# Low halves in VectorE's waits, a row normalised by ScalarE, and eight places of TensorE's side chain moved: a two-layer graph kernel

## The reference

```
q = x[sub] @ Wq.T + bq ; k = x[obj] @ Wk.T + bk          # 8 heads of 64
att[h, e] = (q * k).sum over head h / 8
scores = zeros ; scores[:, sub, obj] = att
scores = where(adj == 0, -inf, scores) ; diagonal = 1e-7
A = softmax(scores, axis=2).sum over heads / 8
x = layernorm(x + A @ x)
x = layernorm(x + adj @ (x @ weight) + bias)
```

## Time and profile before

| what | value |
|---|---|
| median of 3 runs | 165.84 us |
| lowest, highest | 165.1, 166.38 us |
| profiled execution: its own time | 166.42 us |
| profiled execution: span, first to last instruction | 164.7 us |
| busy, share of the span: PE, DVE, ACT, POOL | 93%, 77%, 45%, 43% |
| granted TensorE clock, mean | 0.994 |

### The profile page before, as it was taken

The page is one execution under the profiler, slowest core; times in us unless marked ns, Lnnn a source line. Parts: engine busy times, 40 slices in busy tenths (PEclk is TensorE's granted clock), DMA queues, the critical chain, the costliest instruction groups (busy, mean ns, idle before and its releaser), DMA issues.

```text
span 164.7 us, 2902 instructions
## 1 busy us (share of the span) xinstructions
PE 153.4 (93%) x1024; PEld 79.9 (49%) x1025; DVE 126.9 (77%) x391; ACT 74.0 (45%) x125; POOL 70.5 (43%) x83
## 2 busy tenths in 40 slices
PE   3989999999999999999979999999999999999950
PEld 3934445455454445444434486444665444444530
DVE  2997889994899999999557988798991568666681
ACT  5687459845864412874191044153112104333451
POOL 7588777777777777787604434000020000000000
PEclk9999999999999999999999999999999999999997
DMA  4999889999259999651002730000001992312233
GB/s 124 388 379 343 318 230 336 379 408 364 81 143 358 320 345 380 221 119 39 0 0 49 186 143 6 0 0 0 0 0 24 337 299 106 131 69 71 88 127 127
DMA packets 16232, 28.99 MB, mean 176 GB/s; under 512 B 4769, under 2 KB 5953, under 8 KB 16086
## 3 DMA queue, kind: packets, MB, share of 16 engines
q1 hardware_dynamic: 10742, 24.14, 42.1%
q10 hardware_dynamic: 3280, 3.07, 5.5%
q0 software_dynamic: 2192, 1.57, 4.1%
HBM read 19.83 MB, written 8.58 MB: 173 GB/s over the span
## 4 chain that ended last, share of the span: by engine, by line
PE 38%; POOL 34%; issue 11%; DVE 9%; DMA 3%; ACT 1%; POOLq 0%; DVEq 0%
POOL ed_adj L647 29%; PE acc L1374 15%; PE acc L1464 13%; POOL found L655 5%; PE tr L1464 3%; DMA found<-in_adj,top_i 2%; PE tr L1416 2%; DMA ed_i<-in_pairs 1%; PE acc L1489 1%; DVE st L895 1%; DVE y L831 1%; PE acc L1378 1%; PE tr L1453 1%; ACT y L807 0%; PE tr L1429 0%
## 5 line engine op out<-in xcount | busy, mean ns | idle before, releaser
L647 POOL DMA_INDIRECT ed_adj<-in_adj,ed_idx x47 | 48.5, 1033 | 15.8 <-issue 14.0
L1374 PE MATMUL acc<-adjT,x1s 128*128 128x512 f16 (+1 forms) x240 | 49.3, 354 | 0.0
L1306 PE MATMUL acc<-xs,adjT 128*128 128x512 f16 (+1 forms) x176 | 40.6, 379 | 0.5 <-DVE xs L868 0.5
L1374 PEld LDWEIGHTS acc<-adjT,x1s 128*128 128x128 f16 x240 | 22.8, 98 | 21.1 <-issue 0.2
L1306 PEld LDWEIGHTS acc<-xs,adjT 128*128 128x128 f16 (+1 forms) x176 | 16.3, 98 | 20.0 <-DVE xs L868 2.0
L1464 PE MATMUL acc<-whl,xs 128*128 128x512 f16 (+1 forms) x108 | 23.8, 370 | 0.0
L1464 PEld LDWEIGHTS acc<-whl,xs 128*128 128x128 f16 x108 | 10.5, 98 | 11.8
L1306 PE MATMUL tr<-xs,adjT 128*128 128x512 f16 (+1 forms) x66 | 15.2, 379 | 0.0
L698 ACT CAST adjT<-stage 128x1408 f16<-128x1408 f32 x9 | 12.3, 1362 | 6.0 <-DMA stage<-in_adj_T 5.8
L751 ACT ACTIVATE xs<-acc 128x512 f16<-128x512 f32 (+1 forms) x12 | 6.2, 538 | 11.2 <-PE acc L1378 11.2
L686 POOL DMA_INDIRECT x_dram<-wraw,back_i x1 | 1.3, 1337 | 21.5 <-DVE wraw L1224 21.5
(11 more groups left out here) (283 smaller groups left out, 230.7 us busy)
## 6 DMA issues: line engine op xcount, KB each, us to landing
stage<-in_adj_T SPq DMA_DIRECT2D x9, 704.0 KB, 7.3
x_dram<-x_sb SPq DMA_DIRECT2D x10, 256.0 KB
x_sb<-in_x SPq DMA_DIRECT2D x3, 768.0 KB, 7.2
sums_dram<-y ACTq DMA_DIRECT2D x6, 256.0 KB, 6.7
sums_dram<-xd ACTq DMA_DIRECT2D x5, 256.0 KB, 7.1
x_sb<-x_dram SPq DMA_DIRECT2D x1, 1280.0 KB, 12.2
out<-y SPq DMA_DIRECT2D x5, 256.0 KB, 2.0
stage<-in_adj_T SPq DMA_DIRECT2D x3, 384.0 KB, 5.6
```

The source lines that it names most:

```text
L647: nc.gpsimd.indirect_dma_start(out=ed_adj[0:EP, c:c + 1], out_offset=None, in_=adj_flat, in_offset=bass.IndirectOffsetOnAxis(ap=ed_idx[0:E ...
L1306: last = mm(sum_bank(i)[:, :], adjT[0:width[k], k, i * P:(i + 1) * P], xs[0:width[k], half, k, :], start=(k == 0 and half == 0), stop=(k = ...
L1374: mm(mix_bank(u)[:, 0:j - i], x1s[:, half, k, f * P:(f + 1) * P], adjT[:, k, i:j], start=(k == 0 and half == 0), stop=False)
```

## The change

It has four parts. (a) The bias row's low half and a first quarter of the weight's low half are made by DVE in `top_candidates`, ahead of its wait for the eight gathers; the second quarter stands after L1121, the third ahead of the wait for `dots_done`, the fourth ahead of the wait for `scores_spread`. (b) ACT makes the weight's high half ahead of `mix_high(2)`. (c) The row `kk` is normalised by ACT, between `mix_high(6)` and `mix_high(7)`; DVE computes its scale and shift before `mix_low(6)`. (d) Eight stops of the side chain on PE come later in `MIX_ORDER`: seven by two rows, the eighth (the spread scores) by one; from L1439 on they stand where they stood.

```diff
+        base_shift, base_ready = map(sem, ("base_shift", "base_ready"))
...
-            for u in range(3):
+            for u in range(2):
                 mix_high(u)
             act.wait_ge(w1_loaded, 16)
             nc.scalar.mul(whl[:, 0], w1_raw, WS).then_inc(w1_hi, 1)
+            mix_high(2)
...
             mix_high(6)
+            act.wait_ge(base_shift, 1)
+            nc.scalar.activation(kk, kk, ACT.Identity, bias=st[:, 0, 9:10], scale=st[:, 0, 8:9]).then_inc(base_ready, 1)
             mix_high(7)
...
+            def low_bias():
+
+                dve.wait_ge(bias_split, 1)
+                V.scalar_tensor_tensor(bias_hl[:, 1], bias_row[:, :], WS, bias_hl[:, 0], ALU.mult, ALU.subtract).then_inc(bias_split, 1)
+
+            def low_w1(k):
+
+                dve.wait_ge(w1_hi, 1)
+                V.scalar_tensor_tensor(whl[:, 1, k], w1_raw[:, k], WS, whl[:, 0, k], ALU.mult, ALU.subtract).then_inc(w1_lo, 1)
...
                 steps += 1
+                low_bias()
+                low_w1(0)
                 dve.wait_ge(top_found, 16 * TOP)
...
-            dve.wait_ge(bias_split, 1)
-            V.scalar_tensor_tensor(bias_hl[:, 1], bias_row[:, :], WS, bias_hl[:, 0], ALU.mult, ALU.subtract).then_inc(bias_split, 1)
             mix_low(3)
...
+            low_w1(1)
             dve.wait_ge(xsT_hi, 1)
...
-            dve.wait_ge(w1_hi, 1)
-            V.scalar_tensor_tensor(whl[:, 1], w1_raw, WS, whl[:, 0], ALU.mult, ALU.subtract).then_inc(w1_lo, 1)
             dve.wait_ge(xo_hi, 1)
...
+            low_w1(2)
             dve.wait_ge(dots_done, 1)
...
+            low_w1(3)
             dve.wait_ge(scores_spread, 1)
...
+            dve.wait_ge(slot_root, 1)
+            scale_shift(norm_a).then_inc(base_shift, 1)
             mix_low(6)
...
             mix_low(7)
-            dve.wait_ge(slot_root, 1)
-            step(scale_shift(norm_a))
-            step(V.tensor_scalar(kk, kk, norm_a[:, 8:9], norm_a[:, 9:10], ALU.mult, ALU.add))
             dve.wait_ge(slot_root, 2)
...
             dve.wait_ge(row_ready, 1)
+            dve.wait_ge(base_ready, 1)
...
-            mix_rows(0, 35)
+            mix_rows(0, 37)
             pe.wait_ge(flags_ready, 1)
...
-            mix_rows(59, 64)
+            mix_rows(61, 66)
             pe.wait_ge(qk_read, 1)
...
-            mix_rows(64, 72)
+            mix_rows(66, 73)
             pe.wait_ge(scores_ready, 2)
...
-            mix_rows(72, 95)
+            mix_rows(73, 95)
             pe.wait_ge(shares_ready, 1)
...
-            pe.wait_ge(w1_lo, 1)
+            pe.wait_ge(w1_lo, KF)
```

More of the change, by code:

```diff
@@ L1385, in _ @@
             ahead = pe.mark_branch_hint_location()
-            mix_rows(35, 41)
+            mix_rows(37, 43)
             pe.wait_ge(onehot_ready, 1)
@@ L1392, in _ @@
             mm(tr[1][:, 0:1], ones16[0:EP, :], many16[0:EP, :], start=True, stop=True).then_inc(many_counted, 1)
-            mix_rows(41, 46)
+            mix_rows(43, 48)
             pe.wait_ge(spread_ready, 1)
             mm(tr[0][:, 0:192], ones16[0:64, :], subs16[0:64, 0:192], start=True, stop=True).then_inc(subs_spread, 1)
-            mix_rows(46, 53)
+            mix_rows(48, 55)
             pe.wait_ge(xobj_in, 16)
@@ L1401, in _ @@
             last.then_inc(xobj_T, 1)
-            mix_rows(53, 56)
+            mix_rows(55, 58)
             pe.wait_ge(xsub_in, 16)
@@ L1407, in _ @@
             last.then_inc(xsub_T, 1)
-            mix_rows(56, 59)
+            mix_rows(58, 61)
             def project(bank, n, rows_T):
```

## The result

Over 20 timings of each, the changed kernel took a median of 166.28 us (165.41 to 167.57) against 165.06 us (164.51 to 166.38): a ratio of 1.0067 with an interval of 1.0039 to 1.0094. It is slower, by two thirds of a per cent, where I forecast 0.1% faster. 166.28 lies in my range; the sign was wrong. The profiled execution took 167.29 us (span 165.5), against 166.42 (span 164.7) before: 0.87 us more.

The account below looks back on a forecast made before the run. PE, busy throughout from 115 to 156 us, was taken to bound the kernel, its start set by DVE's shares. DVE's chain gains 0.17, the rows and part c nothing: 165.84 - 0.17 = 165.67, say 165.7 us; range 164.8 to 166.4.

Parts of the forecast that it names:

- About 0.3 of a wait stays: PE at the flags: four moved matmuls fill 0.86 us of its 1.16 us wait; the gathers still set 84.33.
- the 0.58: The sum: median of the runs lies 0.58 us below the profiled time, so 166.25 becomes 165.67.
- I take nothing: Last gather beside part a's two instructions at 80.4: no delay charged, as earlier gathers lost 0.13 us on average.
- the 1.20 that I called the slowest: Gathers beside DVE's two-SBUF-input blocks (71.9 to 77.6): slowest taken as 1.20 us, against 0.95 for the last one.
- The rule of the Trainium skill that I weighed: GpSimd shares SBUF interfaces with VectorE and two SBUF inputs contend; could slow the last gather, speaking against part a.
- The chain: DVE from flags to shares: low-half work removed or moved, quarters added; shares ready 0.17 us sooner, 114.32 for 114.49.
- the rest of the 0.22: Head sums: PE arrives 0.22 us sooner; DVE gains 0.16 and the third quarter eats the remainder.
- The 1.79 of xo: xo's low half on DVE, read as held 1.1 us by POOL's copy; forecast below 0.7 us when moved to 95.9.
- Part c and ACT: Normalised row on ACT at 0.81 us, change ready about 0.8 sooner, no gain; ACT's queue behind base_shift has 0.7 us cover.
- The new wait of 0.7 at the shares: PE at the shares: would naturally arrive at about 113.7 but stops at 114.38, so about 0.7 us of new wait.
- The moved rows: Rival: PE keeps the 0.86 us won at the flags, giving 164.8 us (164.4 to 165.3); chance 0.18.
- The held gather: Rival: DVE's two-SBUF-input instructions at 80.4 to 81.6 delay the last gather 0 to 1.2 us; 166.0 to 166.9, chance 0.12.

Follow-up runs that it names:

- e7: Kernel before with only the moved rows of part d (two rows ahead of the flags): 166.56 us, 1.0039 of the kernel before.
- e11: Kernel before with the first eight stops on PE moved by four rows instead of two: 166.85 us, 1.0057 of the kernel before.
- e2: Changed kernel with only the bias row's low half left in DVE's wait at the gathers: 165.93 us, 1.0033 of the kernel before.
- e3: Changed kernel with only the first quarter of the weight's low half left in DVE's wait at the gathers: 165.94 us, 1.0029 of the kernel before.
- e5: Kernel before plus two extra DVE instructions with two SBUF inputs in the gathers' wait: 165.49 us, 0.9992 of the kernel before.
- e8: Kernel before plus a one-column memset behind each of the first five blocks of x's split on DVE: 165.62 us, 1.0020 of the kernel before.
- e10: Changed kernel with the rows back in their old places (parts a, b, c alone): 165.72 us, 0.9959 of the kernel before.
- e4: Changed kernel with both low halves in the wait but started only after the last gather's issue, by a POOL memset's mark: 166.31 us, 1.0053 of before.
- e12: Changed kernel with mix_low(5), base row and moments behind the shares, ACT's root behind mix_high(6), PE's change stop three rows later: 165.29 us, 0.9966 of before.
- e14: Kernel before plus four extra DVE instructions near the last gathers, one input in PSUM and one in SBUF: 165.64 us, 1.0012 of before.
- e9: Kernel before, unchanged, timed and profiled once more: 166.18 us, 1.0009 of the kernel before.
- e1: Changed kernel with both low halves (bias row and first quarter) taken out of DVE's wait at the gathers: 166.51 us, 1.0058 of the kernel before.
- e15: e12 with e4's mark, so both low halves start only behind the last gather's issue: 166.21 us, 1.0030 of the kernel before.
- e16: e15 with the rows in the places of the kernel before: 165.28 us, 0.9978 of the kernel before.

## Why the prediction was wrong

**What bounds the kernel: right in the method, wrong in its weight.** The end is the shares' stop plus PE's work: from that stop to PE's last matmul 43.96 us in both kernels. But the stop at the shares is, with the old chain, the stop at the flags plus 30.09 to 30.22 us in every profile, but for e7 and e11 with 29.85 and 29.83 (before's chain with moved rows). The number that decides is when PE comes to the flags.

**The step that failed: "About 0.3 of a wait stays, and the flags' matmul still starts at 84.33, because the gathers set it."** It was read from one execution. There the gathers do set it; with part a in place they set it 0.92 later. In the profiles of e2, e3, e5 to e8, e10 and e11 PE comes to the flags after DVE's mark or within 0.06 of it, and there the four matmuls aren't fill but 0.86 us of delay for DVE's chain (four rows in e11 twice that). PE gets it back as matmuls it no longer has in front of the shares, stands there for 0.5 to 0.6 instead, and the end is later. From the start of the products to the shares the changed kernel takes 45.42 us in e2, e3 and e4, 0.80 more than the 44.62 of 35 rows without a wait; of that the rows alone make 0.55 (e7, 45.17). The times agree in direction: e7 1.0039, e11 1.0057, and e10, without the rows, no loss (0.9959). A warning stood in my own numbers: the profiled execution, at 166.42 us, lay above all three timed runs (165.1 to 166.38), and I subtracted the 0.58 without asking which of its waits the others lack.

**Part a at the gathers, "I take nothing": wrong in executions with late gathers.** 1.04 us in the changed kernel's profile and as much in e12's; nothing in e4 (behind the gather) and e14 (one input in PSUM). My reason was that six steps beside the blocks at 71.9 to 77.6 had lost 0.13 us each on average. But there most of the gathers had slipped in between two blocks; the last had no such luck. And the 1.20 that I called the slowest was not: the gather from 77.56, just at the blocks' end, took 1.29, held by a cast. The row that priced it was in the trace I had, and I didn't use it. POOL's third gather and DVE's split of x, before:

```profile
10.07 4.01 POOL L647 DMA_INDIRECT ed_adj<-in_adj,ed_idx  x1 [0.31 <-issue]
```

```profile
9.57 3.68 DVE L868 SCALAR_TENSOR_TENSOR xs<-x_sb,xs 128x512 f16<-128x512 f32 x6
```

10.07 + 4.01 - 0.83 = 13.25 = 9.57 + 3.68: a gather held by six two-input instructions in a row until the last ended. In the early kind it starts at 8.77 or so, the run has only three blocks (in e10 to 10.15), and the gather ends 0.82 behind the third.

The rule of the Trainium skill that I weighed (page "GPSIMD Engine Reference", section "Specifications": the SBUF interfaces are shared with VectorE, and two SBUF inputs contend) agrees with this: 1.99 and 1.98 beside two inputs, 0.94 twice beside one, with the other in PSUM. The casts and copies of a single SBUF input that held gathers too (1.29, 1.44) go beyond what I had drawn from it. I had set my 0.13 above it; that was the wrong choice.

**The chain: right in mechanism, 0.07 for 0.17 in size.** xo's low half at 0.68, ACT's high half as the next stop, the quarter in front of the head sums: all there. What it brought is below what can be timed. And its source was the rows, not part a: with the rows alone and the old block of 2048 columns, e7 and e11 have 29.85 and 29.83, 0.3 less than e5. DVE takes the head sums 17.55 us behind the flags in e7 and 17.71 in e3, where the third quarter stands before them, and the spread scores at 21.24 and 21.50, behind the fourth. So the quarters, priced at nothing here beyond "the rest of the 0.22", cost 0.25 where PE comes late (45.42 for 45.17). The 1.79 of xo was of one execution too: the same kernel in e9 has 0.68, started 0.11 before POOL's copy.

**Part c and ACT: right.** The row took 0.82 on ACT (0.81 foretold), mix_high(7) came behind it, and PE stopped for nothing: 0.81 us of slack at the change.

**The new wait of 0.7 at the shares: right in size (0.58), wrong in meaning.** I took it for gain that is lost again. It is gain lost again only if there was gain; without a wait at the flags it is plain loss.

**The rivals.** The moved rows didn't stay won. That 166.28 lies in my range is due to the spread of the runs that I had added to it, not to the mechanism. The held gather came in at 1.04 of its 1.2 us; by that rival alone the sum was 165.84 - 0.17 + 1.04 = 166.7, and the profiled execution rose by 0.87. The median, 166.28, lies in that rival's range as well, but the hold explains it only for executions with late gathers. What no rival had was the executions in which PE isn't early at all.

**How the 0.67% is made up** is not settled to the tenth. By e7 about 0.4% is the rows, with an interval from nothing to 0.8%. The hold adds its 1.04 us only in executions with late gathers. The 20 times of before fall into 14 up to 165.21 (mean 164.89) and 6 from 165.8 (mean 165.98), those of after into 8 up to 165.91 (165.62) and 12 from 166.26 (166.84): 0.73 and 0.86 later within a group, near the 0.80 of a late PE and the 0.87 of the profiled pair. But the groups are cut by eye (after has a wider gap at 167), a time doesn't tell its kind (e9, with a third gather of 4.01, took 165.74), and why more executions fell into the upper group after the change nothing here shows. e1 and e4, without a hold to be expected, stayed at 1.0058 and 1.0053, and their intervals overlap with those of e2, e3 and e7. Also open is why e15's median lies above e16's and its own best by 1.4 us.

## What to carry to other kernels

A wait read from one profiled execution is fill only if the other executions have it: compare the profiled time with the timed runs, profile the kernel before a second time, and size the fill by the execution with the shortest wait. Work that a later stage hangs on should not stand behind fill of that kind; take slack out of the chain behind it first, then move the rows (e12's and e15's profiles speak for it, the time of e15, 1.0030, doesn't). And a wait of DVE is a free place for an instruction only if it doesn't hold up what DVE is waiting for; put it behind the gather's issue (e4, gather 0.94), or give it a PSUM input (e14, 0.94).

## What the runs showed of the hardware

- An indirect gather of 0.94 to 0.95 us that meets DVE instructions with two SBUF inputs ends 0.82 to 0.83 us after the end of one of them: 1.99 and 1.98 beside two, 4.01 beside six in a row, 2.20 to 2.22 where the row had three. Whether it gets in between two that follow each other isn't fixed: near 10 us it didn't, not even past memsets of one column (e8), and of the single gathers beside the blocks at 75.10 several did. What decides that is open.
- Casts and copies with one input, from SBUF to SBUF, do the same: 1.29 with an end 0.83 after a 64x64 cast (e5), 1.44 with an end 0.82 after a copy of 128x1024 (e9, gather from 78.03, copy from 77.96 for 0.69). Instructions with one input in PSUM and one in SBUF didn't (e14, 0.94 twice).
- It goes the other way too: xo's low half 1.79 begun behind the start of POOL's copy and 0.68 ahead of it, and a DVE instruction of 0.24 took 1.26 when begun 0.14 behind POOL's of 1.30. From the profile before to the one after, POOL's first copy fell from 1.64 to 1.31 us.
- Executions of one kernel differ by more than noise: a third gather of 4.01 or 2.20 us, begun at 10.07 or 8.77, and a start of the products anywhere from 68.2 to 70.4 us.
